# Last batch's table entries made by products of marked places instead of a store, in a decoder kernel on one Trainium2 core

## The chip, the cores and the metric

The kernel runs on one core of a Trainium2 chip. The metric is the device time in microseconds (us) of one execution. A core has a matrix engine (TensorE, in rows PE, its weight loads PEld), VectorE (DVE), ScalarE (ACT), GpSimd (POOL) and a queue of SyncE (SP) that only starts transfers. Each engine works through its own instructions in order; semaphores order them against each other.

## The reference

x has 8 batches of 256 rows of 512 numbers. Three layers follow each other, each added to its input after a layer normalisation:

```
x = x + self_attention(layernorm(x))        # 16 heads of 32, causal
x = x + cross_attention(layernorm(x), ctx)  # keys and values: 256 of ctx, 256 of the rows
xt = layernorm(x).reshape(-1, 512)
probs = softmax(xt @ wg)                    # 8 experts
idx = argmax(probs); gate = probs[idx]
x = x + gate * (W[idx] @ xt + b[idx])       # one 512x512 expert per row
```

The change touches the third layer and its seam with the end of the second.

## The kernel before

Self-attention runs first for all batches, then `cross_attention` batch by batch, in TensorE jobs named by letters: X transposes of the rows, q, k, v products, s scores, p transposes of the probabilities, o values, y output product, Y transposes of the normalised output, l logits of the 8 experts. The last batch has only what is left to do: `LAST = s0 s1 p0 p1 o0 o1 o2 o3 y0 y1 Y0 l0 Y1 l1`. All matrices are split in a high and a low part, and a product is three passes of four matmuls (`three_pass`, L54 to L62): high x high, high x low, low x high. Making the parts is a copy on ScalarE (`high`, `hi_part`) and a subtraction on VectorE or GpSimd (`low`, `lo_part`). The weights of the 8 experts are split between the jobs.

Routing gives each of the 2048 rows ("tokens") its expert and a slot in a table `slots` in memory: 2048 slots for each expert, entries of (token number, gate). For each batch `choose` finds the expert, `count` (five small matmuls) the rank among the tokens of the same expert, `place_tokens` the slot, `gates` the gate, and GpSimd's `store_entries` scatters two times 128 entries. `Blocks` then divides the filled slots in 23 blocks of 128 tokens of one expert. Of batches 0 to 6 alone at least 7 blocks are full (KNOWN = 7): these blocks are known before the last batch is routed (`known_blocks`), the others after it (`other_blocks`).

`Products` computes the blocks, one per step, each engine with its own instructions for step k (block numbers are those of the step unless said):

- SP reads a block's 128 entries from the table into k_tab (L1032); ScalarE turns token numbers into gather and scatter numbers (L1833, L1837); GpSimd gathers the rows of x and of the normalised x by an indirect transfer into one of six places (L1043), and scatters the result (L1804).
- TensorE transposes block k (four, L1867), then multiplies block k-1 with its expert (twelve matmuls, L61).
- ScalarE copies the transposed high part (L1843), VectorE makes the low part of block k (L1932), then finishes block k-1: the product plus the bias (L1922), times the gate plus the rows (L1926).

The entries are read LOOK = 3 blocks ahead, rows are gathered AHEAD = 4 blocks ahead. The order of everything is written out by hand; nothing schedules it anew. Steps 0 to 4 are written out, the other 18 are a loop of six steps run three times. SP reads the entries of block 7 and later only when the last batch's entries have landed.

Of the kernel before, what the change touches and what calls it, by code (L numbers as in the profile page):

```python
# [14 lines left out]
I32 = mybir.dt.int32  # L15
# [38 lines left out]
def three_pass(pe_matmul, out, lhs, rhs, first=True, last=True, before_low=None):  # L54
# [727 lines left out]
class Routing:  # L782
# [8 lines left out]
    def __init__(self, nc, cx):  # L791
        sb = lambda n, s, d=F32: cx.enter_context(nc.sbuf_tensor("r_" + n, s, d))
        sem = lambda n: cx.enter_context(nc.semaphore("r_" + n))
        self.table = nc.dram_tensor("slots", [self.ROWS, 2], I32).ap()
# [14 lines left out]
        self.ranks_done, self.slot_done, self.gsum_done = sem("ranks_done"), sem("slot_done"), sem("gsum_done")  # L809

    CONSTS = 8

    def constants(self, nc, pool):
# [4 lines left out]
        nc.gpsimd.iota(self.entry[:, :, 0], pattern=[[P, TB]], base=0, channel_multiplier=1).then_inc(self.token_done, 1)  # L818
        pool.wait_ge(self.consts, 4)
        pool.wait_ge(self.token_done, 1)  # L820
        nc.gpsimd.tensor_copy(self.rank[:], self.rank_i[:]).then_inc(self.consts, 1)
        nc.gpsimd.tensor_copy(self.next[:], self.next_i[:]).then_inc(self.consts, 1)
        nc.gpsimd.tensor_copy(self.token[:], self.entry[:, :, 0]).then_inc(self.consts, 1)
# [21 lines left out]
    def gates(self, nc, dve, n):  # L845
# [5 lines left out]
        nc.vector.reciprocal(self.entry[:, :, 1].bitcast(F32), self.gsum[:]).then_inc(self.gate_done, 1)  # L851
# [17 lines left out]
    def place_tokens(self, nc, dve, n):  # L869
# [13 lines left out]
        nc.vector.tensor_copy(self.slot_i[:], self.slot[:]).then_inc(self.slot_done, 1)  # L883
# [18 lines left out]
class Blocks:  # L902
# [5 lines left out]
    AHEAD, LOOK = 4, 3  # L908
# [3 lines left out]
    PLACES = (1, 2, 0)  # L912
    REST = COUNT + LOOK - KNOWN
    CONSTS = 9

    def __init__(self, nc, cx, x2n, stage):
# [3 lines left out]
        columns = self.COUNT + self.LOOK  # L920
        self.upto = sb("upto", [P, E, E])
        self.full_i, self.full = sb("full_i", [P, NT], I32), sb("full", [P, NT])
        self.block_i, self.block_no = sb("block_i", [P, columns], I32), sb("block_no", [P, columns])
        self.first_i, self.first = sb("first_i", [P, E], I32), sb("first", [P, E])
        self.number, self.over = sb("number", [P, E]), sb("over", [P, E, NT])
# [1068 lines left out]
```

## Time and profile before

| what | value |
|---|---|
| median of 3 runs | 732.34 us (732.12 to 733.02) |
| profiled execution, its own time | 732.93 us |
| its span | 730.7 us |
| TensorE busy | 665.9 us (91% of the span) |
| VectorE busy | 547.8 us (75%) |
| ScalarE, GpSimd busy | 308.1 us (42%), 314.1 us (43%) |
| TensorE in the chain that ended last | 40%, of it 36% in matmuls of L61 |

The span is from the first to the last recorded instruction. Busy time is an average over stages with different limits, so a view by stretches is needed beside it. The granted clock of TensorE has two levels here, 2.4 GHz (1.0) and 1.2 GHz (0.5). Rows of a timeline give the start, the duration, engine, line, operation, written and read tiles, shape and number of merged instructions; in brackets the idle time ahead and what ended it. Matmuls overlap each other, so the distance of starts says more than durations.

### The profile page before, as it was taken

What the parts mean: (1) busy time and instruction counts of PE and PEld (TensorE: products, weight loads), DVE (VectorE), ACT (ScalarE), POOL (GpSimd) and SP (SyncE); (2) the same over time, 40 slices, a digit from 0 to 9 for tenths busy, and PEclk for the clock granted to TensorE, in tenths of its full rate; (3) what the DMA queues carried; (4) which work ended last, traced back from release to release, by engine and by line L of the source; (5) the groups of instructions that cost most, each with busy time, mean ns of one, the idle gap of its engine ahead of it and who ended that gap; (6) DMA issues with size and microseconds to landing.
All of it is one profiled execution on the core that took longest, in us unless ns stands there. A gap on an engine that the chain in (4) does not pass through costs nothing.

```text
span 730.7 us, 18994 instructions
## 1 busy us (share of the span) xinstructions
PE 665.9 (91%) x5896; PEld 589.3 (81%) x5897; DVE 547.8 (75%) x1659; ACT 308.1 (42%) x990; POOL 314.1 (43%) x543
## 2 busy tenths in 40 slices
PE   4768999999999989898999999999999997589994
PEld 4658788889898978796989898989898986468883
DVE  4776878787877888882678787878787867775663
ACT  3445566566665666661414141414141536212220
POOL 4377666575757677761500101010101241346652
PEclk9889999999999999999999999999999999679997
DMA  6386886666556656871950607060704673577520
GB/s 258 125 176 119 132 137 131 140 123 144 123 136 124 138 114 133 171 148 44 374 197 1 170 3 167 6 172 0 171 1 145 196 202 93 185 162 202 166 85 9
DMA packets 143051, 97.23 MB, mean 133 GB/s; under 512 B 110750, under 2 KB 114974, under 8 KB 142624
## 3 DMA queue, kind: packets, MB, share of 16 engines
q1 hardware_dynamic: 137344, 84.10, 48.2%
q0 software_dynamic: 5664, 12.61, 6.0%
q8 instruction: 21, 0.34, 0.2%
q14 instruction: 22, 0.18, 0.1%
HBM read 58.24 MB, written 18.77 MB: 105 GB/s over the span
## 4 chain that ended last, share of the span: by engine, by line
PE 40%; DVE 3%; DMA 3%; issue 3%; POOL 2%; ACT 1%; SPq 0%; DVEq 0%; ACTq 0%; POOLq 0%
PE b_bank L61 36%; DMA stage<-x2n,k_gather_no 1%; DVE w_lo L1562 1%; PE b_bank L1867 1%; DMA bias_sb<-in_wo 1%; PE b_bank L1464 1%; PE b_bank L1515 1%; POOL w_lo L1351 1%; DMA k_tab<-slots 1%; DVE b_smax L1578 1%; DVE w_lo L1113 0%; ACT w_hi L1391 0%; ACT w_hi L1401 0%; ACT w_hi L1101 0%; ACT b_prob L1408 0%
## 5 line engine op out<-in xcount | busy, mean ns | idle before, releaser
L509 ACT ACTIVATE prob<-prob,shift 128x128 f32<-128x128 f32 (+1 forms) x256 | 114.6, 449 | 116.5 <-POOL shift L420 116.1
L61 PE MATMUL b_bank<-w_hi 128*128 128x256 f32 (+1 forms) x528 | 107.0, 325 | 4.3 <-DVE w_lo L1562 4.0
L61 PE MATMUL a_job<-w_hi 128*128 128x256 f32 (+1 forms) x488 | 95.0, 318 | 15.5 <-DVE w_lo L712 7.2
L1391 ACT CAST w_hi<-b_bank 128x256 fp32r<-128x256 f32 (+1 forms) x128 | 52.9, 450 | 128.1 <-PE b_bank L61 116.9
L61 PE MATMUL b_bank<-w_lo,w_hi 128*128 128x256 f32 (+1 forms) x528 | 104.4, 320 | 0.0
L61 PE MATMUL b_bank<-w_hi,w_lo 128*128 128x256 f32 (+1 forms) x528 | 104.0, 319 | 0.0
L733 DVE CUSTOM_DVE_ANT_0 prob<-a_s,mask 128x128 f32<-128x128 f32 (+1 forms) x256 | 79.8, 348 | 30.1 <-PE a_s L609 30.0
L61 PEld LDWEIGHTS a_job<-w_hi 128*128 128x128 f32 x488 | 71.7, 196 | 25.4 <-DVE w_lo L712 7.8
L61 PEld LDWEIGHTS b_bank<-w_hi 128*128 128x128 f32 x528 | 80.9, 191 | 12.3 <-DVE w_lo L1562 5.4
L741 DVE TENSOR_TENSOR p_part<-prob,p_part 128x384 f16<-128x384 f32 x128 | 78.4, 612 | 13.6 <-POOL p_part L427 11.9
L61 PEld LDWEIGHTS b_bank<-w_lo,w_hi 128*128 128x128 f32 x528 | 82.3, 192 | 7.1
L61 PE MATMUL a_job<-w_lo,w_hi 128*128 128x256 f32 (+1 forms) x488 | 87.9, 303 | 0.0
L61 PEld LDWEIGHTS b_bank<-w_hi,w_lo 128*128 128x128 f32 x528 | 82.1, 192 | 6.9
L61 PE MATMUL a_job<-w_hi,w_lo 128*128 128x256 f32 (+1 forms) x488 | 87.2, 302 | 0.0
L1562 DVE TENSOR_TENSOR w_lo<-b_bank,w_hi 128x256 fp32r<-128x256 f32 (+1 forms) x128 | 62.7, 512 | 25.4 <-ACT w_hi L1391 25.2
L420 POOL TENSOR_SCALAR shift<-nmax 128x2 f32<-128x2 f32 x128 | 44.2, 346 | 84.9 <-DVE nmax L733 80.4
L61 PEld LDWEIGHTS a_job<-w_lo,w_hi 128*128 128x128 f32 x488 | 72.6, 196 | 3.0
L61 PEld LDWEIGHTS a_job<-w_hi,w_lo 128*128 128x128 f32 x488 | 72.3, 195 | 2.9
L427 POOL CAST p_part<-prob 128x384 f16<-128x384 f32 x128 | 64.4, 503 | 12.9 <-DMA pt<-p_part 4.2
L1613 DVE CUSTOM_DVE_ANT_0 b_unwanted<-xn_sb,bias_sb 128x512 bf16<-128x512 f32 x96 | 64.1, 687 | 3.1 <-DVE xn_sb L1547 1.9
L712 DVE TENSOR_TENSOR w_lo<-a_job,w_hi 128x256 fp32r<-128x256 f32 (+1 forms) x92 | 43.3, 478 | 18.5 <-ACT w_hi L496 18.1
L509 ACT ACTIVATION_READ_ACCUMULATOR prob<-prob,shift 128x1 f32 x256 | 48.2, 188 | 0.0
(191 smaller groups left out, 1115.2 us busy)
## 6 DMA issues: line engine op xcount, KB each, us to landing
stage<-in_w SPq DMA_DIRECT2D x6, 1024.0 KB, 7.2
xin<-in_x SPq DMA_DIRECT2D x8, 512.0 KB, 4.4
xr<-in_x SPq DMA_DIRECT2D x8, 512.0 KB, 4.0
x<-xr SPq DMA_DIRECT2D x8, 512.0 KB, 3.2
xin<-x SPq DMA_DIRECT2D x8, 512.0 KB, 9.7
stage<-in_ctx_t SPq DMA_DIRECT2D x8, 512.0 KB, 3.6
stage<-in_ctx SPq DMA_DIRECT2D x8, 512.0 KB, 5.3
xr<-x SPq DMA_DIRECT2D x8, 512.0 KB, 6.3
```

The source lines that it names most:

```text
L61: ins = pe_matmul(out, a, b, start=first and i == 0, stop=last and i == len(steps) - 1)
L420: nc.gpsimd.tensor_scalar(shift[:, e, :], nmax[:, e, :], LN_UNIT, None, ALU.add).then_inc(shift_done, 1)
L427: nc.gpsimd.tensor_copy(p_part[:, t % NPROB, 0, :], prob[:, t % NPROB, :]).then_inc(p_hi_done, 1)
L509: a = nc.scalar.activation(prob[:, e % NPROB, cols], prob[:, e % NPROB, cols], ACT.Exp, scale=-1.0, bias=shift[:, e, q:q + 1], accum_out=r ...
L712: nc.vector.tensor_tensor(lo, src, hi, ALU.subtract).then_inc(job_ev, 1)
L733: m = nc.vector.tensor_tensor_reduce(out=prob[:, s % NPROB, cols], in0=s_ps[s % HG][:, q, 0:P * (q + 1)], in1=mask[:, P * (1 - q):], scale ...
L741: nc.vector.tensor_tensor(p_part[:, t % NPROB, 1, :], prob[:, t % NPROB, :], p_part[:, t % NPROB, 0, :], ALU.subtract).then_inc(p_done, 1)
L1351: nc.gpsimd.tensor_tensor(wt_lo["o"], wo_raw, wt_hi["o"].bitcast(F32), ALU.subtract).then_inc(wo_split, 1)
L1391: nc.scalar.copy(hi, src).then_inc(job_hi, 1)
L1464: m = nc.tensor.transpose(b[:, c * P:(c + 1) * P], src[:, i, c * P:(c + 1) * P], ident[:])
L1562: nc.vector.tensor_tensor(lo, src, hi.bitcast(F32), ALU.subtract).then_inc(job_ev, 1)
L1613: nc.vector.tensor_tensor_reduce(out=unwanted[:, i % 2, :], in0=xn3_sb[:, t, :], in1=wg_all[:, e, :], scale=1.0, scalar=0.0, op0=ALU.mult, ...
```

## The change

The last batch's entries are not stored in the table. The table and everything read from it is f32 now instead of int32, so that numbers can be added; unused slots hold 2048 and gate 0. For every block from number 7 on:

- VectorE marks (`last_tokens`): for each of the last batch's two groups of 128 tokens a 128x128 tile `here` of zeros and ones, one where a token's slot (`routing.slot`) equals the block's first slot (`blocks.at`) plus a place 0 to 127 (`blocks.place`).
- TensorE multiplies (`fresh_entries`): `here` of each group with the group's entries (128x2: token minus 2048 minus slot as stored by `place_tokens`, and gate), summed in PSUM. It is in the tile r_ranks.
- VectorE adds the result to the entries read from the table (`whole_entries`), and ScalarE's gather numbers wait for that.

The marks of block k+4 stand at the end of VectorE's step k; TensorE multiplies those of block k+3 in its step k, between transposes and product.

Moved besides: Y1, l0 and l1 of the last batch stand within the twelve matmuls of product 0, with tile 1's normalisation, the moves of Y0 and Y1, `choose`, `gates` and `place_tokens` in VectorE's steps 0 and 1; `known_blocks`, `place_tokens` and `gates` of batch 6 stand earlier in the last batch; the entries of the 7 known blocks are read in one go; the gathers of blocks 0 to 5 are issued ahead (AHEAD = 6), four of them around the two rstd operations; expert 6 is loaded into xin and xn, expert 7 into x2_sb and xn3_sb once these are stored, and its low parts are made in VectorE's step 4; there are three product banks instead of two; 11 steps are written out, and the loop of six runs twice.

```diff
 def three_pass(pe_matmul, out, lhs, rhs, first=True, last=True, before_low=None, behind=None):
...
+        if behind and i in behind:
+            behind[i]()
...
     def place_tokens(self, nc, dve, n, last=False):
...
-        nc.vector.tensor_copy(self.slot_i[:], self.slot[:]).then_inc(self.slot_done, 1)
+        if last:
+            nc.vector.scalar_tensor_tensor(self.entry[:, :, 0], self.entry[:, :, 0], float(-B * S), self.slot[:], ALU.add,
+                                           ALU.subtract).then_inc(self.change_done, 1)
+        else:
+            nc.vector.tensor_copy(self.slot_i[:], self.slot[:]).then_inc(self.slot_done, 1)
...
-    AHEAD, LOOK = 4, 3
+    AHEAD, LOOK = 6, 3
...
-        LAST = "s0 s1 p0 p1 o0 o1 o2 o3 y0 y1 Y0 l0 Y1 l1".split()
+        LAST = "s0 s1 p0 p1 o0 o1 o2 o3 y0 y1 Y0 Y1 l0 l1".split()
...
             blocks.first_gather(nc, pool, tick_pool, experts, 0)
             blocks.first_gather(nc, pool, tick_pool, experts, 1)
+            rstd_tile(0)
+            blocks.first_gather(nc, pool, tick_pool, experts, 2)
+            blocks.first_gather(nc, pool, tick_pool, experts, 3)
+            rstd_tile(1)
+            pool.wait_ge(xn3_ready, B * TB)
+            experts.low(nc.gpsimd, 6, (0, 1))
...
-        sp.wait_ge(routing.entries_in, 16 * NT)
         sp.wait_ge(blocks.at_done, 1)
...
+        within_first = {DC: lambda: last_job("Y1"), 2 * DC: last_logits}
+
+        def fresh_entries(i, k):
+            pe.wait_ge(self.here_done, TB * self.fresh(i, k))
+            pe.wait_ge(routing.change_done, 1)
+            for t in range(TB):
+                m = nc.tensor.matmul(routing.fresh_ps[:, k % RX, :], self.here[:, k % 2, t, :], routing.entry[:, t, :],
+                                     start=t == 0, stop=t == TB - 1)
+            m.then_inc(self.fresh_done, 1)
 
         def step(i, k):
             transposes(i, k)
-            if isinstance(i, int) and k == 0:
+            if k + LOOK >= KNOWN:
+                fresh_entries(i, k + LOOK)
+            if k >= 1:
+                product(i, k - 1, within_first if isinstance(i, int) and k == 1 else None)
+            if isinstance(i, int) and k == 1:
                 routing.count(nc, pe, B - 1)
-            if k >= 1:
-                product(i, k - 1)
...
-        LOWS = {0: (6, (0, 1)), 1: (6, (2, 3)), 2: (7, (0, 1)), 3: (7, (2, 3))}
+        LOWS = {2: (6, (2, 3)), 4: (7, range(DC))}
+
+        def last_tokens(i, k):
+            if isinstance(i, int) and k == KNOWN:
+                dve.wait_ge(blocks.place_done, 2)
+            if not isinstance(i, int) or k >= KNOWN + 2:
+                dve.wait_ge(self.fresh_done, self.fresh(i, k) - 2)
+            for t in range(TB):
+                nc.vector.tensor_scalar(self.here[:, k % 2, t, :], blocks.place[:], column_of(blocks.at, i, k),
+                                        routing.slot[:, t:t + 1], ALU.add, ALU.is_equal).then_inc(self.here_done, 1)
+
+        def whole_entries(i, k):
+            dve.wait_ge(self.fresh_done, self.fresh(i, k))
+            dve.wait_ge(tab_in[k % RX], (turn(i, k) + 1) * 16)
...
+            nc.vector.tensor_tensor(at, routing.fresh_ps[:, k % RX, :], at, ALU.add).then_inc(self.whole_done, 1)
...
+            if isinstance(i, int) and k in behind_low:
+                behind_low[k]()
+            if isinstance(i, int) and k == 1:
+                blocks.other_blocks(nc, dve, routing)
+            if k + LOOK >= KNOWN:
+                whole_entries(i, k + LOOK)
+            if k >= 1:
+                finish(i, k - 1)
             if isinstance(i, int) and k in LOWS:
                 experts.low(nc.vector, *LOWS[k])
-            if isinstance(i, int) and k == 1:
-                blocks.other_blocks(nc, dve, routing)
-            if k >= 1:
-                finish(i, k - 1)
+            if k + LOOK + 1 >= KNOWN:
+                last_tokens(i, k + LOOK + 1)
```

TensorE, one step of the loop, kernel before (b_bank<-ident,stage are the transposes, L61 the product):

```order
L61 MATMUL b_bank<-w_lo,c_xt_hi 128x512
L61 MATMUL b_bank<-w_hi,c_xt_lo 128x512 x4
L1867 MATMUL b_bank<-ident,stage 128x128 [waits c_xt_done,k_rows_in4]
L1867 MATMUL b_bank<-ident,stage 128x128 x3
L1875 ISA
L1875 TENSOR_LOAD k_owner_i
L1875 ISA x2
L1877 REGISTER_ALU
L1878 ISA [waits c_xt_done]
L61 ISA [waits c_bias_done,e_split]
L61 MATMUL b_bank<-w_hi,c_xt_hi 128x512
```

TensorE, the same place in the changed kernel (r_ranks<-r_entry,b_prob are the two entry matmuls, b_prob the marks):

```order
L65 MATMUL b_bank<-w_hi,c_xt_lo 128x512 x4
L1922 MATMUL b_bank<-ident,stage 128x128 [waits c_xt_done,k_rows_in4]
L1922 MATMUL b_bank<-ident,stage 128x128 x3
L1950 REGISTER_ALU
L1953 MATMUL r_ranks<-r_entry,b_prob 128x2 [waits r_change_done,c_here_done]
L1953 MATMUL r_ranks<-r_entry,b_prob 128x2
L1930 ISA
L1930 TENSOR_LOAD k_owner_i
L1930 ISA x2
L1932 REGISTER_ALU
L1933 ISA [waits c_xt_done]
```

Between transposes and product two matmuls have come in that wait for c_here_done, and the product's own instructions are queued behind them.

VectorE, one step of the loop, kernel before (c_xt_lo is the low part, xr<-b_bank,bias_sb and the row of L1926 are finish):

```order
L1932 TENSOR_TENSOR c_xt_lo<-b_bank,c_xt_hi 128x512 [waits c_xt_hi_done]
L1915 ISA
L1915 TENSOR_LOAD k_owner_i
L1915 ISA x2
L1918 ISA
L1922 ISA [waits c_y_done,c_out_done0]
L1922 TENSOR_TENSOR xr<-b_bank,bias_sb 128x512
L1926 ISA [waits c_bias_done]
L1926 SCALAR_TENSOR_TENSOR xr<-xr,k_tab,stage 128x512
```

VectorE, the same place in the changed kernel (b_prob<-b_unwanted,k_at_no,r_slot are the marks; the tile b_unwanted holds the places 0 to 127):

```order
L2025 TENSOR_TENSOR c_xt_lo<-b_bank,c_xt_hi 128x512 [waits c_xt_hi_done]
L1999 ISA [waits c_fresh_done,k_tab_in4]
L1999 TENSOR_TENSOR k_tab<-r_ranks,k_tab 128x2
L2006 ISA
L2006 TENSOR_LOAD k_owner_i
L2006 ISA x2
L2013 ISA [waits c_y_done,c_out_done3]
L2013 TENSOR_TENSOR xr<-b_bank,bias_sb 128x512
L2017 REGISTER_ALU [waits c_bias_done]
L2019 ISA [waits c_whole_done]
L2019 SCALAR_TENSOR_TENSOR xr<-xr,k_tab,stage 128x512
L1991 ISA [waits c_fresh_done]
L1991 TENSOR_SCALAR b_prob<-b_unwanted,k_at_no,r_slot 128x128 x2
```

The addition to k_tab has come in ahead of finish, and the two marks behind it; they are the last work of the step.

GpSimd, around the last batch's first gathers, kernel before (b_rstd are the two tiles' normalisation, stage<-x2n the gathers):

```order
L1374 TENSOR_TENSOR b_rstd<-b_veps,b_expo 128x1 [waits b_ln3_dve,xn3_out,x2_out]
L1374 TENSOR_TENSOR b_rstd<-b_veps,b_expo 128x1 [waits b_ln3_dve]
L1043 DMA stage<-x2n,k_gather_no 128x1024 [waits e_split,k_first_no_done]
L1043 DMA stage<-x2n,k_gather_no 128x1024 [waits k_first_no_done]
L1043 DMA stage<-x2n,k_gather_no 128x1024 [waits e_split,k_first_no_done]
L1043 DMA stage<-x2n,k_gather_no 128x1024 [waits k_first_no_done]
L890 DMA slots<-r_entry,r_slot_i 17792x2 [waits r_gate_done,r_slot_done]
L890 DMA slots<-r_entry,r_slot_i 17792x2
```

GpSimd, the same place in the changed kernel:

```order
L1067 DMA stage<-x2n,k_gather_no 128x1024 [waits k_first_no_done,e_split,x2_out,xn3_out]
L1067 DMA stage<-x2n,k_gather_no 128x1024 [waits k_first_no_done]
L1408 TENSOR_TENSOR b_rstd<-b_veps,b_expo 128x1 [waits b_ln3_dve]
L1067 DMA stage<-x2n,k_gather_no 128x1024 [waits e_split,k_first_no_done]
L1067 DMA stage<-x2n,k_gather_no 128x1024 [waits k_first_no_done]
L1408 TENSOR_TENSOR b_rstd<-b_veps,b_expo 128x1 [waits b_ln3_dve]
L1137 TENSOR_TENSOR w_lo<-xin,w_hi 128x512 [waits e_split,e_hi_done,b_xn3_ready]
L1137 TENSOR_TENSOR w_lo<-xin,w_hi 128x512
L1067 DMA stage<-x2n,k_gather_no 128x1024 [waits e_split,k_first_no_done]
L1067 DMA stage<-x2n,k_gather_no 128x1024 [waits k_first_no_done]
```

The gathers of blocks 0 and 1 have moved ahead of the first rstd, those of 2 and 3 between the two, those of 4 and 5 behind a part of expert 6; the store of the entries is gone.

## Rows read from the trace of the kernel before

**Rows 1.** The page, part 2: granted TensorE clock, tenths, in 40 slices.
```profile
PEclk9889999999999999999999999999999999679997
```

**Rows 2.** Windows: length, busy us of PE, PEld, DVE, ACT, POOL; PEclk, DMA share, GB/s.
```profile
600.00:659.10 59.10, 45.17 (x209) 36.46 (x209) 42.63 (x117) 18.99 (x36) 17.62 (x20) 0.80 0.55 143
...
659.10:720.40 61.30, 61.30 (x301) 49.74 (x299) 38.25 (x56) 13.92 (x55) 35.45 (x36) 1.00 0.45 138
...
628.00:640.00 12.00, 7.51 (x35) 6.29 (x36) 8.57 (x26) 1.38 (x3) 4.32 (x5) 0.50 0.84 275
...
655.00:658.00 3.00, 3.00 (x8) 2.32 (x8) 0.69 (x1) 0.18 (x2) 0.00 (x0) 0.50 0.63 217
```

**Rows 3.** Timeline, TensorE, a step of the products: start, us, instructions.
```profile
665.60 0.60 PE L1867 MATMUL b_bank<-ident,stage 128*128 128x128 f32 x4
...
665.96 1.18 PE L61 MATMUL b_bank<-w_hi,c_xt_hi 128*128 x4
...
668.85 0.60 PE L1867 MATMUL b_bank<-ident,stage 128*128 128x128 f32 x4
```

**Rows 4.** Timeline, VectorE, the same step.
```profile
669.22 0.69 DVE L1922 TENSOR_TENSOR xr<-b_bank,bias_sb 128x512 f32<-128x512 f32 x1 [1.03 <-PE b_bank L61]
...
670.08 0.75 DVE L1926 SCALAR_TENSOR_TENSOR xr<-xr,k_tab,stage 128x512 f32<-128x512 f32 x1 [0.16 <-DVE xr L1922]
...
670.74 0.68 DVE L1932 TENSOR_TENSOR c_xt_lo<-b_bank,c_xt_hi 128x512 fp32r<-128x512 f32 x1
```

**Rows 5.** Timeline, TensorE, last batch and first blocks; idle time in brackets.
```profile
618.47 1.16 PE L61 MATMUL b_bank<-w_hi,c_xt_hi 128*128 128x512 f32 x4 [1.11 <-DVE c_xt_lo L1562]
...
627.07 0.74 PE L1464 MATMUL b_bank<-ident,xn_sb 128*128 128x128 f32 x4 [2.78 <-DVE xn_sb L1666]
...
629.28 1.85 PE L1515 MATMUL b_bank<-b_wg,b_prob 128*128 128x8 f32 x8 [1.46 <-DVE b_prob L1594]
...
639.32 2.07 PE L61 MATMUL b_bank<-w_hi,c_xt_hi 128*128 x4 [1.77 <-DVE c_xt_lo L1932]
...
644.57 0.60 PE L1867 MATMUL b_bank<-ident,stage 128*128 128x128 f32 x4
...
653.70 0.66 PE L1867 MATMUL b_bank<-ident,stage 128*128 128x128 f32 x4 [1.89 <-DMA stage<-x2n,k_gather_no]
...
654.67 2.01 PE L61 MATMUL b_bank<-w_hi,c_xt_hi 128*128 x4 [0.31 <-issue]
...
659.11 0.60 PE L1867 MATMUL b_bank<-ident,stage 128*128 128x128 f32 x4
```

**Rows 6.** Timeline, GpSimd: token step behind the stored entries; first gather.
```profile
621.36 0.22 POOL L896 TENSOR_SCALAR r_token<-r_token 128x2 f32<-128x2 f32 x1 [6.99 <-DMA slots<-r_entry,r_slot_i]
...
627.52 1.15 POOL L1043 DMA_INDIRECT stage<-x2n,k_gather_no  x1 [0.18 <-issue]
```

**Rows 7.** Timeline, VectorE, last batch and block 1's step.
```profile
618.43 0.29 DVE L963 TENSOR_TENSOR k_over<-k_number,k_full 128x128 f32<-128x128 f32 x1
...
622.01 0.75 DVE L1589 SCALAR_TENSOR_TENSOR x_sb<-b_bank,b_rinv,xr 128x512 f32<-128x512 f32 x1
...
636.16 1.29 DVE L1113 TENSOR_TENSOR w_lo<-bias_sb,w_hi 128x512 fp32r<-128x512 f32 x2
...
642.00 0.16 DVE L1011 TENSOR_TENSOR k_number<-r_next,k_first 128x8 f32<-128x8 f32 x1
...
645.19 0.18 DVE L986 TENSOR_SCALAR k_owner_i<-k_owner 128x19 int32<-128x19 f32 x1
```

**Rows 8.** Timeline, TensorE: the logits of batch 6 at full clock.
```profile
598.39 1.85 PE L1515 MATMUL b_bank<-b_wg,b_prob 128*128 128x8 f32 x16
```

**Rows 9.** Timeline, VectorE: tile 0 of the last batch normalised.
```profile
626.38 0.55 DVE L1666 TENSOR_SCALAR xn_sb<-x_sb,b_mv,b_rstd 128x512 f32<-128x512 f32 x1
```

**Rows 10.** Timeline, TensorE: first o part of the last batch.
```profile
609.87 0.77 PE L61 MATMUL b_bank<-w_hi 128*128 128x256 f32 x4 [1.45 <-DVE w_lo L1562]
```

**Rows 11.** Timeline, TensorE: the last product.
```profile
717.45 1.09 PE L61 MATMUL b_bank<-w_hi,c_xt_hi 128*128 x4
```

More of the change, by code:

```diff
@@ L51, in batch_rows, with three_pass @@
     return rows.rearrange("(t p) n -> p t n", p=P)
-def three_pass(pe_matmul, out, lhs, rhs, first=True, last=True, before_low=None):
+def three_pass(pe_matmul, out, lhs, rhs, first=True, last=True, before_low=None, behind=None):
     (lh, ll), (rh, rl) = lhs, rhs
@@ L982, in positions @@
         else:
-            m = nc.vector.tensor_tensor(at_i, base, at_sum, ALU.add)
+            at = self.at[:, self.KNOWN:]
+            then(nc.vector.tensor_tensor(at, base, at_sum, ALU.add))
+            m = nc.vector.tensor_copy(at_i, at)
         m.then_inc(at_done, 1)
@@ L1045, in gather, with first_numbers @@
                                 bounds_check=batches * S - 1, oob_is_err=False).then_inc(self.rows_in[k % self.RX], 16)
-    def first_numbers(self, nc, act):
-        for k in range(self.AHEAD):
+    def first_numbers(self, nc, act, blocks):
+        for k in blocks:
             act.wait_ge(self.tab_in[k], 16)
@@ L1325, in _ @@
             load_bias(0)
-            for k in range(Blocks.AHEAD, Blocks.KNOWN):
-                blocks.entries(sp, routing.table, 0, k)
+            for stored in x2n_out:
+                sp.wait_ge(stored, 16 * B)
+            sp.wait_ge(job_done, done_at("Y1", B - 1))
+            experts.load(sp, w, 7)
             products.sync(sp)
@@ L1368, in _ @@
             routing.next_tokens(nc, pool, tick_pool, B - 2)
+            pool.wait_ge(dots_done, (B - 2) * TB * E)
+            blocks.places(nc, pool, unwanted[:, 1, 0:2 * P].bitcast(I32), unwanted[:, 0, 0:2 * P].bitcast(F32))
             for stored in x2n_out:
@@ L1428, in _ @@
             batch(B - 1)
-            act.wait_ge(job_done, done_at("y1", B - 1))
-            experts.high(nc, act, 7)
-            blocks.first_numbers(nc, act)
+            blocks.first_numbers(nc, act, range(4))
+            experts.high(nc, act, 6)
+            blocks.first_numbers(nc, act, range(4, Blocks.AHEAD))
             products.act(act)
@@ L1518, in batch @@
             def batch(n):
-                for j in order(n):
+                for j in order(n)[:order(n).index("Y0") + 1] if order(n) is LAST else order(n):
                     job(j, n)
-                    if j == ("o3" if order(n) is not LAST else "s1") and has_routing(n):
+                    if j == ("o3" if order(n) is not LAST else "s0") and has_routing(n):
                         routing.count(nc, pe, n - 1)
@@ L1869, in transposes, with product @@
             t.then_inc(t_done, 1)
-        def product(i, k):
+        def product(i, k, behind=None):
             m = number_of(i, k)
```

199 lines of the change are left out of this document (114 added, 85 removed).

## The prediction

> **What bounds the kernel now.** I read the page's busy rows first, then windows over the end of the program, and last the timeline of TensorE and VectorE there. TensorE is busy for nine tenths of the span, at full clock in nearly every slice; near the end slices of lower clock stand [rows 1]. The windows say where: between 600 and 659.1 us TensorE is busy for 45.2 of 59.1 us, and from 628 to 640 its granted clock is 0.50; but from 659.1 to 720.4 it is busy for 61.3 of 61.3 us at clock 1.00 [rows 2]. So the end has two parts with different limits. In the first (last batch and first blocks) TensorE waits for other engines. In the second it is itself the limit: each step of the products issues four transposes and twelve matmuls, and the next step's transposes stand 3.25 us behind (665.60, 668.85) [rows 3].
>
> In that second part VectorE lags TensorE, and nobody minds. The product that starts at 665.96 is picked up by VectorE at 669.22, 3.26 us later; its add stands until 670.08, its multiply-add until 670.74, then the low parts follow [rows 3, 4]. TensorE meanwhile computes the next product, which needs nothing of these results.
>
> **The head, where the change gains.** In TensorE's rows [rows 5] these waits stand: 2.78 us before Y0's transposes at 627.07, 1.46 before the first logits, 1.77 before the first product at 639.32, and 1.89 before block 4's transposes at 653.70, which come late because a gather waited for its table entries. The change answers all: last-batch entries are no longer stored, gathers 0 to 3 go out before the rows of Y1, and logits and Y1 stand within product 0.
>
> Step by step, on the clock of this trace. The entries of batch 6 landed 7 us behind their issue, at 621.36, and the table could be read only then; the first gather followed at 627.52 [rows 6]. The small operations that make these entries stood behind the p parts, at 609.7 to 610.8; now they follow s0's maximum, some 4.5 us earlier. The operations that find the known blocks (618.43 to 622.01 and one of 0.2 us ahead, 3.8 us [rows 7]) move ahead of o0, together with two of the four w_lo of expert 3. VectorE then has 0.15 + 3.8 + 1.3 + 0.8 + 1.3 + 0.8 us from about 609.8, which ends at 618.0; before, the last o part began at 617.90. y0 starts no later than 618.5. The first gather can be issued at about 620.5 instead of 627.52 [rows 6] and lands before Y0 is done. rstd for tile 0 is behind two gathers of 1.3 us each, free at 623.1 against veps at 624.1: hidden. tile 0 is normalised directly behind its statistics and one w_lo, at about 625, so Y0 starts near 625.7, 1.4 us earlier.
>
> Product 0 now needs only blocks' rows and one low part, which VectorE gives behind the second tile's statistics (628.5 + 0.7): start at 629.4, 10 us earlier than 639.32. But its surroundings are dear. It runs at half clock, as everything did from 628 to 644 [rows 2]: 12 matmuls 5.3 us (639.32 to 644.57), Y1 0.8, logits 3.7 (twice the row of 1.85 [rows 5]), so it ends near 639. Then VectorE chooses, places (about 2.3 us of small operations) and finds the other blocks (3.5 us, from 642.00 to the end of k_owner_i at 645.4 [rows 7]), finishes block 0 (1.5), and only then makes the low part of block 2: 646.0. Block 2's product starts at 646.5 and block 4's transposes at about 649.6, against 653.70. The head is worth 4.1 us at block 4; I allow 5 us either way, since six waits were chained.
>
> **The added work in the loop.** From step 4 on, TensorE gets for each block two f32 matmuls of 128x128 by 2 columns. The trace has the like: the logits of batch 6 at full clock, 16 instructions for 8 calls in 1.85 us [rows 8]; so four instructions cost 0.46 us. VectorE gets two TENSOR_SCALAR of 128x128. The nearest rows are 0.29 us (128x128, two tensors) and 0.55 (128x512 with two scalars) [rows 7, 9]; with the first as the upper price of one, the pair costs between 0.29 (fully overlapped) and 0.58, and I take 0.4. The addition to the table's entries is 0.17, while VectorE waits anyway.
>
> **The wait that decides.** The order rows of the changed kernel show it. On VectorE the two marks stand last in a step, behind the multiply-add of finish. On TensorE the matmuls that wait for these marks stand behind the transposes and ahead of the product. Count the numbers: step k of VectorE marks block k+4 behind finish(k-1); step k of TensorE multiplies block k+3, whose marks are those of VectorE's step k-1, behind finish(k-2). finish(k-2) needs product k-2, which is the last thing that TensorE did. Between that product and its own next one TensorE has only four transposes. So the lag which was free becomes a loop through both engines:
> - product start to VectorE's add: 3.26 us; add 0.86; multiply-add 0.66 [rows 3, 4]: 4.78;
> - two marks 0.4; one more wait 0.05; resumption of TensorE 0.12 (xn_sb ends at 626.93, transposes start 627.07 [rows 5, 9]);
> - entry matmuls and the issue of the product behind them: 0.85. The stalled transposes at 653.70 had their product 0.97 us behind them, with 0.31 of "issue" [rows 5], where without stall it is 0.36; two calls fewer are there now.
>
> Sum 6.2 us a step at full clock, against 3.24 (bounds 5.9 and 6.5). What is queued behind the waiting matmul is the whole product; VectorE, ScalarE and the gathers wait for that in turn. In step 4 the w_lo of expert 7 (four, 2.6 us by [rows 7]'s 1.29 for two) stand ahead of the marks and add 2.6 us.
>
> **The clock.** Each step leaves TensorE idle for some 2.1 us between transposes and entries, and 0.4 more behind them. In this trace a wait of 1.89 us with a short burst in it was followed by half clock from 655 to 658, one of 2.78 likewise, and one of 1.45, with another close ahead of it, as well; one of 1.11 was not [rows 2, 5, 10]. The step with the fall at 655 took 5.41 us (653.70 to 659.11); less 3.24 and the 0.31 of issue, the fall cost 1.9. If every gap brought it a step would be 8.1 us, if none 6.2; if the clock never came back 9.0 (product 5.25 instead of 2.89, entries 0.46 more). Uninterrupted matmuls of one product brought the clock back twice, by the products of 639.32 and 654.67 [rows 5], and each step holds one of 2.9 us at full or 5.3 at half clock. I take a fall in half of the steps: 7.15 us.
> The Trainium skill (TensorE: Matmul & The Clock Gate, section on HAM oscillation) names as harmful only idle gaps longer than these 2.1 us. By that rule the clock would stay full and the time would be that of the first rival below; the rows at 655 disagree with it.
>
> **The sum.** Steps 4 to 22 are 19. Span = 649.6 (block 4's transposes) + 2.6 + 19 x p + 2.9 (the last product) + 10.35 (from its end at 720.35 to 730.7, the product having started at 717.45 [rows 11]; the last scatter is unchanged). The same way of counting gives the old span back: 653.70 + 5.41 + 18 x 3.25 + 2.9 + 10.35 = 730.9. With p = 7.15 the span is 801.3. The profiled execution took 732.93 for a span of 730.7, and the median is 0.6 lower; so 1.6 comes on top: 803 us, 9.6% slower.
>
> **The rivals.**
> - Same loop, clock never falls (p = 6.2): 783.3 + 1.6 = 785. For it: 2.1 us is close to the smallest wait that was followed by a fall, and the entries' matmuls interrupt it. Against: the row of 1.89.
> - Same loop, clock stays at half (p = 9.0): 836.5 + 1.6 = 838. For it: from 628 to 644 it stayed there through waits no longer than these. Against: one full product brought it back both times.
> - The marks come in time after all, because VectorE gets a step ahead while TensorE is in the head. Then TensorE is the bound with 3.24 + 0.48 = 3.72 a step: 649.6 + 70.7 + 13.25 + 1.6 = 735, about the same as before, since 19 x 0.48 = 9 us eat the head's gain. Against: finish cannot be ahead of its product, by the order rows.
> - The other side, faster: the marks are in time and the entry matmuls of 2 columns slip into the weight loads' shadow (3.3 us a step); block 4 at 646. Then 646 + 62.7 + 13.25 + 1.6 = 723.5. It decides from the point where TensorE's row shows no wait ahead of r_ranks. For it: PEld is busy for 49.7 of 61.3 us only [rows 2]. Against: the logits' row, where such matmuls took 0.116 us each.
>
> **Chances.** Forecast 0.58; full clock 0.17; half clock 0.10; marks in time 0.09; faster 0.06. The forecast alone spans 785 to 822 us. The range is 767 to 837: it leaves out the two cases with the marks in time (0.15) and a sliver at the top. About 0.2%, 1.5 us, is what a measurement can tell from no change. Faster by more: 0.06 and 0.02 of the case at 735; within: 0.03; slower: 0.89.
>
> **What would show it.** In the changed profile each step of the loop should have TensorE idle for about 2 us ahead of r_ranks<-r_entry, released by VectorE's b_prob<-b_unwanted marks; VectorE's add should start 3.3 us behind the product's start, or 5.5 at half clock; the steps should be 6.2 to 9 us apart with the granted clock falling in some; product 0 should start near 629 and block 4 near 650. The prediction is wrong if TensorE has no idle time in the loop, or if its steps are 3.7 us apart.

## The result, and the profile of the changed kernel

| what | before | changed |
|---|---|---|
| median | 732.38 us (732.12 to 733.02, 4 runs) | 809.25 us (808.53 to 816.64, 4 runs) |
| ratio | 1 | 1.1055, 95% interval 1.1022 to 1.1089 |
| profiled execution, its span | 732.93, 730.7 us | 809.41, 807.7 us |

The page of the changed kernel, its busy rows and the granted clock (tenths, 40 slices):

```profile
PE 699.2 (87%) x5972; PEld 612.6 (76%) x5973; DVE 560.1 (69%) x1717; ACT 310.0 (38%) x991; POOL 317.3 (39%) x547
...
PEclk9879999999999999999999999999999986889778
```

The slices near the end differ from [rows 1]: there the clock was 9 again behind the dip at the last batch, but for the last slice; now seven of the last eight slices stand below 9. Windows over that end (length, busy us of PE, PEld, DVE, ACT, POOL; PEclk, DMA share, GB/s):

```profile
628.00:640.00 12.00, 10.04 (x61) 7.88 (x60) 8.97 (x37) 2.24 (x8) 5.17 (x6) 1.00 0.97 360
640.00:647.80 7.80, 4.46 (x13) 3.53 (x14) 5.27 (x9) 2.65 (x5) 3.27 (x3) 0.78 0.54 168
647.80:797.20 149.40, 103.79 (x393) 80.54 (x391) 55.99 (x122) 16.74 (x58) 35.68 (x36) 0.82 0.19 61
```

From 628 to 640 the clock is 1.00 where it was 0.50, and TensorE is busy for 10.0 us, not 7.5 [rows 2]. In the loop of products, where it had been busy without a break (from 659.1 on, [rows 2]), it now works 104 of 149 us at a mean clock of 0.82. TensorE's timeline shows both parts; first the head:

```profile
626.31 0.63 PE L1504 MATMUL b_bank<-ident,xn_sb 128*128 128x128 f32 x4 [1.72 <-DVE xn_sb L1706]
...
629.63 1.19 PE L65 MATMUL b_bank<-w_hi,c_xt_hi 128*128 x4 [1.12 <-DVE c_xt_lo L2025]
...
632.03 1.85 PE L1555 MATMUL b_bank<-b_wg,b_prob 128*128 128x8 f32 x16
...
643.34 2.07 PE L65 MATMUL b_bank<-w_hi,c_xt_hi 128*128 x4 [3.48 <-DVE c_xt_lo L2025]
...
647.78 0.60 PE L1922 MATMUL b_bank<-ident,stage 128*128 128x128 f32 x4
```

Product 0 starts at 629.63 instead of 639.32, the logits lie within it at full clock, and block 4's transposes start 5.9 us earlier than those of [rows 5]. Then one early step, the step of expert 7's low parts, and two of the loop:

```profile
650.13 0.61 PE L1953 MATMUL r_ranks<-r_entry,b_prob 128*128 128x2 f32 x4 [1.76 <-DVE b_prob L1991]
651.09 1.19 PE L65 MATMUL b_bank<-w_hi,c_xt_hi 128*128 x4 [0.35 <-DVE c_xt_lo L2025]
...
653.98 0.60 PE L1922 MATMUL b_bank<-ident,stage 128*128 128x128 f32 x4
658.81 1.02 PE L1953 MATMUL r_ranks<-r_entry,b_prob 128*128 128x2 f32 x4 [4.23 <-DVE b_prob L1991]
...
664.50 0.60 PE L1922 MATMUL b_bank<-ident,stage 128*128 128x128 f32 x4
...
709.18 0.60 PE L1922 MATMUL b_bank<-ident,stage 128*128 128x128 f32 x4
711.76 0.61 PE L1953 MATMUL r_ranks<-r_entry,b_prob 128*128 128x2 f32 x4 [1.98 <-DVE b_prob L1991]
712.91 1.19 PE L65 MATMUL b_bank<-w_hi,c_xt_hi 128*128 x4 [0.54 <-DVE c_xt_lo L2025]
...
715.81 0.60 PE L1922 MATMUL b_bank<-ident,stage 128*128 128x128 f32 x4
718.46 1.01 PE L1953 MATMUL r_ranks<-r_entry,b_prob 128*128 128x2 f32 x4 [2.05 <-DVE b_prob L1991]
719.62 2.07 PE L65 MATMUL b_bank<-w_hi,c_xt_hi 128*128 x4
...
724.90 0.78 PE L1922 MATMUL b_bank<-ident,stage 128*128 128x128 f32 x4
```

Read the distance from one group of transposes to the next: 6.20 us from 647.78, 10.52 behind it, 6.63 from 709.18, 9.09 from 715.81 (at half clock: the product's first four rows take 2.07 us, not 1.19), against 3.25 in [rows 3]. Each has the same wait, for VectorE's marks; the loop of six begins at 702.67, the steps ahead of it are written out. VectorE in that first step:

```profile
648.08 0.69 DVE L2013 TENSOR_TENSOR b_prob<-b_bank,bias_sb 128x512 f32<-128x512 f32 x1 [1.80 <-PE b_bank L65]
648.81 0.75 DVE L2019 SCALAR_TENSOR_TENSOR b_prob<-b_prob,k_tab,stage 128x512 f32<-128x512 f32 x1
649.48 0.60 DVE L1991 TENSOR_SCALAR b_prob<-b_unwanted,k_at_no,r_slot 128x128 f32<-128x128 f32 x2
649.99 0.68 DVE L2025 TENSOR_TENSOR c_xt_lo<-b_bank,c_xt_hi 128x512 fp32r<-128x512 f32 x1
```

VectorE waits 1.80 us for the product, then adds, multiplies and marks; only then may TensorE go on. Each engine waits for the other once a step. TensorE's second wait, 0.35 us ahead of the product at 651.09, stands behind a low part (c_xt_lo) in the brackets, but that is block 4's; this product is block 3's, whose low part was made at 645.60, so it is not the low part that holds it.

**Where the 77.0 us of span went.** Between the transposes of block 4 and the last block's lie 18 steps: 60.50 us before (653.70 to 714.20), 139.85 now (647.78 to 787.63), so 79.35 more. The head gives back 5.92. Behind the last transposes 20.07 us are left instead of 16.50, since one more wait and entry stand there: 3.57 more. 79.35 - 5.92 + 3.57 = 77.0. The 60.50 us before hold a stall of their own, the step of 5.41 us at block 4 [rows 5], 2.2 us over the others.

### The profile page after: what moved, and what is told of

Same layout as the page of the kernel before. It is cut to its first block, busy times and chain, and to the rows that moved or that the text cites. A ratio compares the mean times of both kernels' runs of the same rounds, so it can differ in the third digit from the quotient of the medians.

```text
span 807.7 us, 19227 instructions
## 1 busy us (share of the span) xinstructions
PE 699.2 (87%) x5972; PEld 612.6 (76%) x5973; DVE 560.1 (69%) x1717; ACT 310.0 (38%) x991; POOL 317.3 (39%) x547
## 4 chain that ended last, share of the span: by engine, by line
PE 38%; DVE 7%; issue 5%; DMA 2%; POOL 2%; DVEq 1%; ACT 1%; SPq 0%; ACTq 0%; POOLq 0%
PE b_bank L65 35%; PE r_ranks L1953 2%; DVE b_prob L1991 1%; DVE xr L2013 1%; DVE w_lo L1602 1%; DMA bias_sb<-in_wo 1%; DMA slots<-r_entry,r_slot_i 1%; PE b_bank L1504 1%; DVE b_prob L2013 1%; POOL w_lo L1382 1%; DVE xr L2019 1%; DVE b_smax L1618 0%; PE b_bank L1555 0%; DVE w_lo L1137 0%; DVE b_prob L2019 0%
## 5 line engine op out<-in xcount | busy, mean ns | idle before, releaser
L1067 POOL DMA_INDIRECT stage<-x2n,k_gather_no x23 | 24.1, 1048 | 90.5 <-ACT c_scatter_no L1886 86.5
```

Source lines behind the costliest of these rows:

```text
L1067: pool.indirect_dma_start(self.rows(k, slice(0, 2 * D)), None, self.x2n[0:batches * S, :], bass.IndirectOffsetOnAxis(ap=self.gather_no[:, ...
```

## The experiments

Each time stands beside a median of the kernel before that ran on the same chip: 734.12 us (731.36 to 736.41) for e1 to e4, 732.90 (729.59 to 737.79) for e5, e6, f1 and f2, 733.59 (726.46 to 736.04) for g1 and g2. The ratios are to these medians; where a time is set against the changed kernel's 809.25 us, the two are medians of different runs, and a difference of a few us between them is not resolved.

### e1_marks_ahead: the marks ahead of finish on VectorE

```diff
+            if k + LOOK + 1 >= KNOWN:
+                last_tokens(i, k + LOOK + 1)
             if k >= 1:
                 finish(i, k - 1)
...
-            if k + LOOK + 1 >= KNOWN:
-                last_tokens(i, k + LOOK + 1)
```

> The changed kernel, with VectorE's two marks ahead of finish instead of behind it; same instructions otherwise. Theory (the loop product -> finish -> marks -> entry matmuls -> product sets the steps): the marks of block k+4 are then ready a product early, TensorE shows no wait ahead of r_ranks, steps 4 to 22 fall from 7.6 us on average to 3.7 to 3.9 us (3.25 plus 0.48 for the entry matmuls), granted clock 1.00 in the loop; time 809 - 19 x 3.8 = 737 us (734 to 742). Rival (the added work on the two engines, or TensorE's clock for another reason, sets the steps): at most 10 us less, above 795.

Measured: 737.50 us (734.64 to 738.48), ratio 1.0041 (1.0019 to 1.0064). TensorE's timeline:

```profile
659.10 0.61 PE L1953 MATMUL r_ranks<-r_entry,b_prob 128*128 128x2 f32 x4 [1.22 <-DVE b_prob L1991]
...
663.04 0.60 PE L1922 MATMUL b_bank<-ident,stage 128*128 128x128 f32 x4
663.48 0.51 PE L1953 MATMUL r_ranks<-r_entry,b_prob 128*128 128x2 f32 x4
663.85 1.18 PE L65 MATMUL b_bank<-w_hi,c_xt_hi 128*128 x4
...
666.72 0.60 PE L1922 MATMUL b_bank<-ident,stage 128*128 128x128 f32 x4
```

Window over its loop (columns as above):

```profile
649.10:725.70 76.60, 74.37 (x393) 61.73 (x391) 54.23 (x123) 16.68 (x58) 40.85 (x37) 1.00 0.39 121
```

The work is that of the changed kernel, two instructions stand elsewhere, and 72 of 77 us are gone. But for one wait behind expert 7's low parts nothing stands ahead of the entries, the step is 3.68 us (3.67 to 3.93 in the loop of six), and the clock is 1.00 for the whole stretch. So the position of the marks is the cause; 0.43 us a step is what the entry matmuls themselves cost. The 18 steps take 70.02 us. Even so the span is 5.5 us longer than before the change (736.2 against 730.7): block 4 comes 4.6 us earlier (649.10), the 18 steps take 9.5 more, and what stands behind them 0.6 more. The entries cost more than the head gives.

### e2_entries_last: TensorE's entry matmuls behind the product

```diff
-            if k + LOOK >= KNOWN:
-                fresh_entries(i, k + LOOK)
             if k >= 1:
                 product(i, k - 1, ...)
+            if k + LOOK >= KNOWN:
+                fresh_entries(i, k + LOOK)
```

> The changed kernel, with TensorE's entry matmuls behind the product of the step instead of ahead of it; VectorE's order is untouched. Theory: they then wait for marks that were ready a product ago, steps 3.7 to 3.9 us, time 737 us (734 to 745), the same as with the marks moved. Rival (VectorE's order or its added work is what matters): no gain, above 795, since VectorE's instructions are the same.

Measured: 746.91 us (746.01 to 747.32), ratio 1.0178 (1.0135 to 1.0222). The other end of the same wait, and 62 us gone. It keeps 9 us more than e1: in the loop of six most steps are 4.1 to 4.5 us and one is 4.92, where e1 has 3.7 to 3.9, with idle time that the profile puts down to issue. There is a wait of 2.19 us for the marks at 658.22 behind expert 7's parts with half clock behind it, and two short ones in the loop (0.81 us at 687.72, 0.52 at 713.78). So its slack is smaller, and the marks are just late twice; the wait of every step is gone in both.

### e3_filler: eight dummy matmuls in the wait

```diff
             if k + LOOK >= KNOWN:
+                for _ in range(8):
+                    nc.tensor.matmul(self.spare[:, :], wt_hi[:, 0, 0:P], wt_hi[:, 0, 0:D], start=True, stop=True)
                 fresh_entries(i, k + LOOK)
```

> The changed kernel, with eight more matmuls of 512 columns (1.9 us at full clock, their result is not used) between the transposes and the entry matmuls of each step from 4 on, where TensorE waits. Theory on the clock (half clock follows the wait of each step): granted clock 1.00 throughout the loop, steps 6.3 to 6.7 us instead of 7.6, time 809 - 19 x 1.1 = 788 us (782 to 794), faster although more is computed. Rival (the clock falls for another reason, or half clock costs nothing here): same time or up to 19 x 1.9 = 36 us more, 809 to 845.

Measured: 791.14 us (789.85 to 791.96), ratio 1.0788 (1.0742 to 1.0834). More work, 18 us less time. The window over its loop (columns as above) and one step:

```profile
646.90:777.60 130.70, 117.25 (x545) 90.87 (x543) 55.97 (x122) 16.77 (x58) 35.69 (x36) 0.99 0.22 70
```

```profile
669.63 0.60 PE L1923 MATMUL b_bank<-ident,stage 128*128 128x128 f32 x4
669.99 2.08 PE L1962 MATMUL b_bank<-w_hi 128*128 128x512 f32 x8
672.06 0.61 PE L1954 MATMUL r_ranks<-r_entry,b_prob 128*128 128x2 f32 x4
673.02 1.19 PE L65 MATMUL b_bank<-w_hi,c_xt_hi 128*128 x4 [0.36 <-DVE c_xt_lo L2028]
...
675.90 0.60 PE L1923 MATMUL b_bank<-ident,stage 128*128 128x128 f32 x4
```

The step is 6.27 us, as in the changed kernel at full clock (6.20), and 6.6 to 6.75 in the loop; but the mean clock is 0.99, not 0.82. The 18 steps take 121.13 us, not 139.85. That splits the 79.35 us that these steps got longer: the clock 139.85 - 121.13 = 18.7 us, the loop through both engines 121.13 - 70.02 = 51.1, the rest 70.02 - 60.50 = 9.5. The rest is the entries (0.43 x 18 = 7.7) and e1's own waits, less the stall of 2.2 us that the kernel before had. One wait of 2.38 us with half clock behind it is left in e3, in the step of expert 7's parts (10.23 us), so 18.7 is what the dummies took away and a little less than the whole price of the clock.

### e4_marks_between: the marks between finish's two operations

```diff
                 .then_inc(bias_done, 1)
+            if between:
+                between()
             dve.wait_ge(bias_done, m + 1)
```

(`between` is the step's `last_tokens`, which no longer stands behind finish.)

> The changed kernel, with the two marks between the add and the multiply-add of finish, 0.67 us nearer to the product. Theory: each step is 0.67 us shorter plus what the shorter wait gives back in clock: 809 - 19 x 0.67 = 796 us at an unchanged share of half clock, down to 780 if the clock falls more rarely. Rival (VectorE's total work, not its order, sets the steps): no change, 809.

Measured: 793.66 us (792.62 to 795.07), ratio 1.0818 (1.0769 to 1.0866).

```profile
670.33 0.60 PE L1922 MATMUL b_bank<-ident,stage 128*128 128x128 f32 x4
671.96 0.61 PE L1953 MATMUL r_ranks<-r_entry,b_prob 128*128 128x2 f32 x4 [1.03 <-DVE b_prob L1991]
...
675.82 0.60 PE L1922 MATMUL b_bank<-ident,stage 128*128 128x128 f32 x4
677.45 0.61 PE L1953 MATMUL r_ranks<-r_entry,b_prob 128*128 128x2 f32 x4 [1.03 <-DVE b_prob L1991]
678.41 1.20 PE L65 MATMUL b_bank<-w_hi,c_xt_hi 128*128 x4 [0.35 <-issue]
...
682.65 0.82 PE L1922 MATMUL b_bank<-ident,stage 128*128 128x128 f32 x4
```

The multiply-add's 0.7 us left the loop: 5.49 us a step at full clock instead of 6.20. This bears out that a step is the sum of the rows round the loop. The clock still falls, with waits of only 0.85 to 1.04 us: the second step here took 6.83, and 14 of its 18 steps took over 6.8.

### e6_filler_4: four dummy matmuls instead of eight

```diff
-                for _ in range(8):
+                for _ in range(4):
```

> The changed kernel with 4 dummy matmuls of 512 columns (not part of the reference's computation) ahead of each block's entry matmuls, where e3_filler had 8. At full clock they fill 0.85 us of the wait of 1.8 to 2.0 us, so that TensorE idles 1.0 to 1.1 us a step. Theory: the idle time left is that of e4_marks_between (1.03 us), where the clock still fell in nearly every other step; so the mean clock stays near 0.95 and the time between 800 and 809 us, with full-clock steps of 6.2 to 6.6 us as without. Rival: it's the longest gap that decides and 1.0 us in a longer step is short enough: the clock stays up and the time is e3_filler's, 790 to 792 us.

Measured: 796.74 us (795.23 to 797.97), ratio 1.0874 (1.0827 to 1.0920). Neither was right: it lies between. The wait that is left is 0.83 to 0.91 us in the first steps, and one such is followed by a fall (the third row takes 1.81 us, not 1.19), others are not:

```profile
670.65 1.17 PE L1962 MATMUL b_bank<-w_hi 128*128 128x512 f32 x4
672.72 0.61 PE L1954 MATMUL r_ranks<-r_entry,b_prob 128*128 128x2 f32 x4 [0.90 <-DVE b_prob L1994]
673.68 1.81 PE L65 MATMUL b_bank<-w_hi,c_xt_hi 128*128 x4 [0.35 <-DVE c_xt_lo L2028]
...
714.37 0.61 PE L1954 MATMUL r_ranks<-r_entry,b_prob 128*128 128x2 f32 x4 [1.12 <-DVE b_prob L1994]
715.69 1.20 PE L65 MATMUL b_bank<-w_hi,c_xt_hi 128*128 x4 [0.72 <-DVE c_xt_lo L2028]
```

Four of 18 steps took 7.8 us or more (one of them with a wait of 3.30 us behind expert 7's parts), where the changed kernel had eleven over 7.5 and e3 one. With none, four and eight dummies the mean clock over the loop is 0.82, 0.94 and 0.99. From the second step of the loop of six on, e6's waits are 1.00 to 1.12 us, as long as e4's or longer, and one of the eleven was followed by a fall (the last rows: 1.12 us, and the product behind it at full clock); e4's clock over the same stretch is 0.81. So the length of the gap alone does not decide. What does is not isolated: e6 has four more matmuls in a step.

### e5_low_behind_marks: marks ahead of expert 6's and 7's low parts

```diff
+            if k + LOOK + 1 >= KNOWN:
+                last_tokens(i, k + LOOK + 1)
             if isinstance(i, int) and k in LOWS:
                 experts.low(nc.vector, *LOWS[k])
```

> The changed kernel with one move on VectorE: in the steps where expert 6's and 7's low parts are made, the marks come ahead of them, not behind. Theory: the one wait of 4.23 us ahead of the entry matmuls falls to the 1.8 to 2.0 us of its neighbours, and the time by 2.2 us and the half clock that followed it there, 805 to 807.5 us. Rival: the four parts then stand ahead of the next block's copy from PSUM, which comes later by what VectorE's idle time of that step (about 3 us) doesn't hold; the wait moves to the next step and the time stays at 808 to 810 us.

Measured: 812.76 us (806.91 to 815.51), ratio 1.1078 (1.1017 to 1.1139). The wait of 4.23 us has become 1.47; the first row is the wait of the step ahead of it:

```profile
649.58 0.85 PE L1953 MATMUL r_ranks<-r_entry,b_prob 128*128 128x2 f32 x4 [1.75 <-DVE b_prob L1991]
...
658.28 0.61 PE L1953 MATMUL r_ranks<-r_entry,b_prob 128*128 128x2 f32 x4 [1.47 <-DVE b_prob L1991]
659.40 1.56 PE L65 MATMUL b_bank<-w_hi,c_xt_hi 128*128 x4 [0.51 <-DVE w_lo L1137]
```

The first three steps take 24.3 us against 25.4, but all three now see a fall of the clock, and the 18 steps take 139.95 us, as without the edit (139.85). The first step shows how open the clock is: its wait is 1.75 us where the changed kernel's was 1.76, yet it is followed by half clock (8.59 us) and the other was not (6.20). What TensorE had done before differs: in e5 the product ahead had run at full clock (from 644.33), in the changed kernel it had begun at half clock (643.34) and ended at full. The time lies above both forecasts and nearer to the rival's: the local gain of 1.1 us does not reach the end. Its spread of 8.6 us leaves a gain or loss of a few us open.

### f1_bf16_entries and g1_two_parts: cheaper entry matmuls

```diff
-                m = nc.tensor.matmul(routing.fresh_ps[:, k % RX, :], self.here[:, k % 2, t, :], routing.entry[:, t, :],
-                                     start=t == 0, stop=t == TB - 1)
+                for part in range(3):     # 2 in g1
+                    m = nc.tensor.matmul(routing.fresh_ps[:, k % RX, :], self.here[:, k % 2, t, :],
+                                         routing.parts[:, t, part, :], start=t == 0 and part == 0,
+                                         stop=t == TB - 1 and part == 2)
```

(on top of e1; GpSimd makes the bfloat16 parts of the entries once; in g1 the last part is 1, not 2)

> Marks ahead of VectorE's finish as in e1_marks_ahead, and TensorE's entry matmuls in bfloat16: GpSimd splits the entries once into three bfloat16 parts that sum to them, the marks are written as bfloat16, and a block takes 12 small matmuls of 2 columns instead of 4 float32 ones. Theory: what is left of the change's price in e1 is the float32 entry matmuls alone, 3.68 us a step against 3.25 before, so 0.43 x 19 = 8 us, given in part by the stores that are gone; if bfloat16 matmuls of 2 columns take about 0.05 us each, a step falls to some 3.4 to 3.5 us and the time to 737.5 - 19 x 0.25 = 733 us (730 to 736), ratio to before 0.995 to 1.003. Rival A, what costs is the loading of the marks as weights and the number of matmuls, not their type: 12 of them take as long as 4, 737 to 739 us. Rival B, GpSimd's split comes late and holds the first entry matmul back: a wait of some us at the first row of r_ranks, 739 us or more.

> As f1_bf16_entries, but the entries are split into two bfloat16 parts, not three (the sum then has 16 bits of an entry, enough for a token's number; the gate loses its last bits): 4 small matmuls a block, as many as e1's float32 ones, in place of f1's 6. In f1 the steps without a wait took 3.48 us, but about every second one 3.7 to 4.1 us, with 0.16 to 0.44 us of idle time put down to issue ahead of the product. Theory, these waits come with the number of TensorE's instructions in a step, and 4 per block is e1's number, which ran without them in its written-out steps: clean steps of about 3.38 to 3.45 us and few waits, some 0.25 x 18 = 4.5 us less than e1, 732 to 734 us, ratio 0.997 to 1.000. Rival A, the waits for issue are the loop's own and stay when matmuls get short, since TensorE runs out of its queue sooner: 735 us as f1, ratio 1.003. Rival B, the gate's lost bits matter not to the time at all; nothing else in the kernel changes, so a time above 737 would mean that GpSimd's split is what holds the first entries.

Measured: f1 735.46 us (733.51 to 737.52), ratio 1.0035 (1.0014 to 1.0057); g1 734.83 us (732.72 to 737.44), ratio 1.0015 (0.9994 to 1.0037). g1:

```profile
676.09 0.60 PE L1940 MATMUL b_bank<-ident,stage 128*128 128x128 f32 x4
676.53 0.24 PE L1972 MATMUL r_ranks<-r_parts,b_prob 128*128 128x2 bf16 x4
677.17 1.19 PE L65 MATMUL b_bank<-w_hi,c_xt_hi 128*128 x4 [0.40 <-issue]
...
680.07 0.60 PE L1940 MATMUL b_bank<-ident,stage 128*128 128x128 f32 x4
```

f1 has three parts for each of two groups, six matmuls a block, not the twelve of its forecast. Its time is at the upper end of the theory's, its ratio just outside. The clean steps are as short as the theory said, 3.48 in f1 and 3.43 in g1 against e1's 3.68. But about every second step has 0.16 to 0.44 us of idle time put down to issue ahead of the product and takes 3.6 to 4.1. The 18 steps take 69.8 us in f1 and 69.3 in g1, e1's 70.0: nearly all of 0.2 to 0.25 x 18 = 3.6 to 4.5 us is given back. g1 has e1's number of matmuls and the waits all the same, so the number is not their cause. Its rival A was right that they come when the matmuls get short; that they are the loop's own is not so, since one stands in a written-out step of either kernel (0.44 us at 666.02 in f1, 0.23 at 666.25 in g1). What they are, register work or the fetch of instructions, the profile does not say.

### f2_spread and g2_two_parts_lows: VectorE's extra work spread

```diff
-        LOWS = {2: (6, (2, 3)), 4: (7, range(DC))}
+        LOWS = {4: (7, (0,)), 5: (7, (1,)), 6: (7, (2,)), 7: (7, (3,))}
...
-            if isinstance(i, int) and k == 1:      # f2 alone
+            if isinstance(i, int) and k == 2:
                 blocks.other_blocks(nc, dve, routing)
```

(expert 6's two parts go to GpSimd; f2 is on top of f1, g2 on top of g1)

> As f1_bf16_entries, and VectorE's extra work spread: expert 6's two low parts go to GpSimd behind its first gathers, expert 7's four low parts to one a step in steps 4 to 7 instead of four in step 4, and the other batches' marks go from step 1 to step 2. Theory: in e1 one wait of 1.22 us is left at 659.10 behind expert 7's four parts, and the head of the stage waits 3.5 us for the third block's copy; both are VectorE's queue, so 1.2 us and 1 to 1.8 us go: f1 less 2 to 3 us, near 730 us. Rival A: the waits move to the next step or to another operand (the low part itself, late for its expert's product), and the time is f1's within 1 us. Rival B: GpSimd's low parts delay the gathers behind them, f1 plus 1 to 3 us.

> As g1_two_parts, with expert 7's low parts one a step in steps 4 to 7 and expert 6's two on GpSimd, but the other batches' marks left in step 1 (f2_spread had moved them too, and there a wait of 2.25 us ahead of the first entries, at half clock behind it, ate the 2.5 us that the head had won). Theory: the wait of 1.4 us behind expert 7's four parts goes and nothing takes its place: g1 less 1.2 to 1.5 us, 731 to 732 us. Rival: the low parts, spread, lengthen four steps of VectorE and the wait returns in pieces: g1 within 0.7 us.

Measured: f2 735.57 us (734.68 to 738.29), ratio 1.0040 (1.0019 to 1.0060); g2 734.21 us (732.48 to 737.98), ratio 1.0005 (0.9991 to 1.0020). f2 at block 4:

```profile
645.00 0.60 PE L1941 MATMUL b_bank<-ident,stage 128*128 128x128 f32 x4
647.85 0.30 PE L1973 MATMUL r_ranks<-r_parts,b_prob 128*128 128x2 bf16 x6 [2.25 <-DVE b_prob L2012]
648.84 1.20 PE L65 MATMUL b_bank<-w_hi,c_xt_hi 128*128 x4 [0.69 <-issue]
```

Block 4 comes 2.5 us earlier than in f1, and the marks, which need the operations moved from step 1, are then late by 2.25 us, with half clock behind it: the step takes 8.0 us, and the wait has moved, as its rival A said. g2 leaves those in step 1: no wait for marks is left in the loop, its 18 steps take 67.2 us against g1's 69.3, but its block 4 comes 1.0 us later (649.03, not 648.05). In the steps the theory holds (1.4 us of wait gone, 2.1 us less in all); in the time it is the rival's number, since the head gives half of that back. 0.6 us less in the median is inside the intervals. g2 has the lowest median of all versions; neither it nor g1 can be told from the kernel before, and none is shown to beat it.

## Why the prediction was right

By its own steps:

- **The wait that decides: right.** The marks behind finish, and the entries ahead of the product, make a loop through both engines. The step at full clock was 6.20 in the written-out steps (647.78 to 653.98), forecast 6.2; e1 and e2 show the cause from either end, e4 that the rows round the loop add up.
- **The size of its parts.** The marks took 0.60 us as a pair (649.48 to 650.08), forecast 0.4, and the entries followed 0.05 us behind, forecast 0.17; the entries' start to the product's was 0.96, forecast 0.85. From add to multiply-add it was 0.73 where 0.86 was forecast, so the parts' misses nearly cancel in the 6.2. Idle time ahead of the entries was 1.43 to 2.05 us but for the 4.23, and behind them 0.35 to 0.64 in steps at full clock, forecast 2.1 and 0.4. In the program's loop steps at full clock took 6.5 to 6.7, which I had not seen coming: 0.4 more than the 6.20 written out. Half of it lies on VectorE, from the start of the add to that of the multiply-add (0.95 us at 709.49, 0.73 at 648.08), half on TensorE, from the entries to the product (1.15 us at 711.76, 0.96 at 650.13). That it is the loop's register work is argued, not tested.
- **The clock: the mechanism was right, and two misses cancelled in its size.** Falls in 11 of 18 steps, forecast half; by e3 18.7 us, so 1.7 a fall, forecast 1.9. The total was forecast as 0.95 x 19 = 18, and that it came so near is partly luck. The mean p is (807.7 - 10.6 - 2.9 - 2.6 - 647.8) / 19 = 7.57, forecast 7.15. The missing 0.42 x 19 = 8 us are the mis-sized term of the sum, and little of it is the clock. Against 6.2 a step, e3's steps hold 5.0 us more in the 11 that lie in the loop of six, and 2.0 more in the written-out ones beyond the 2.6 of expert 7's parts, mostly in the step with those parts, which keeps its half clock; the last step, 6.59 us, adds 0.4, and the clock 0.7. The traces again disagree with the rule of the Trainium skill (TensorE: Matmul & The Clock Gate, section on HAM oscillation), by which only idle gaps longer than any of these lower the clock: waits of 0.9 to 2.05 us brought half clock in many of the steps, and filling them (e3) took it away.
- **The head: the gain right, its path not.** The first gather went out at 620.50 (forecast 620.5) and product 0 at 629.63 (629.4). The step that failed is "It runs at half clock, as everything did from 628 to 644": the clock was 1.00, the logits 1.85 us, not 3.7. The wait ahead of Y0 was 1.72 us where 2.78 had stood [rows 5]; that this kept the clock up is not tested, and neither is which of the moves in the head won its 5.9 us. Of what this won, product 2's wait of 3.48 us with half clock behind it took some back, so block 4 came at 647.8, forecast 649.6: 1.8 us, within the 5 allowed.
- **Expert 7's low parts.** The wait of 4.23 us against 1.76 is 2.5 more, forecast 2.6. That taking it away gives 2.5 back is not so (e5): where the clock falls and returns, what one step gained was lost in its neighbours.
- **Entries at 0.48 us.** e1's 3.68 against 3.25 gives 0.43. The third rival, 735 us, is near what e1 measured (737.5): with the marks in time, that is the time. The faster rival's premise, entries hidden by the weight loads, does not hold: with the marks in time no step was below 3.67 us in e1, and none below 3.42 with the shorter matmuls of g1 and g2.

The sum, 803 against 809.25, is off by 6 us: +8 for p, -1.8 for the head, +0.25 for the tail (10.6, forecast 10.35). The head's error, of the other sign, hid a part of p's.

## What to carry to other kernels

Before an operation of one engine is put behind another engine's newest result, number the steps: if B's operation in step k follows the result of A's last work, and A's next work waits for B, the time of a step becomes the sum of both paths, not the larger. Such an operation belongs ahead of what waits (here two lines higher, worth 72 us). And look at what the new gap does to TensorE's clock: here it cost 18.7 us beyond the idle time itself. Price the added work too where the engine that gets it is the limit: 0.43 us in each of 18 steps was more than the 4.6 to 5.9 us that the change won ahead of them.

## What the hardware showed that was not expected

- Eight matmuls that compute nothing made the kernel 18 us faster (809.25 to 791.14), by holding the mean clock of the loop at 0.99 instead of 0.82.
- Gaps of 0.90 us (e6) to 1.03 us (e4) in steps of 5.5 to 6.3 us were followed by half clock; near-equal gaps (0.83 to 1.12 us in e6 but for one, 0.85 to 1.04 in e4) gave a mean clock of 0.94 in the one and 0.81 in the other. One and the same wait, 1.75 and 1.76 us, was followed by half clock in e5 and not in the changed kernel.
- Making TensorE's small matmuls shorter (0.51 to 0.24 us a group) brought idle time put down to issue, 0.16 to 0.44 us in about every second step, and so gained 0.7 of 4.5 us.
